# Routing 13 sequences ahead of the attention, and the experts' sums beside its last steps

## The chip, the cores and the metric

The kernel runs on one core of a Trainium2 chip. Measured is the device time of one execution, in microseconds; given is the median over runs. The core's engines are TensorE (PE in the profile; PEld are its weight loads), VectorE (DVE), ScalarE (ACT), GpSimd (POOL) and SyncE (SP). Each works through its own list of instructions in order, and they wait for one another by semaphores. SyncE only issues transfers here; GpSimd and ScalarE can issue some too. All transfers run on the core's 16 DMA engines.

## The reference, cut to what matters

Two layers follow each other on 32 sequences of 256 tokens with 128 features. Layer 0 (a Mamba block and a gated feed-forward) is not touched. Layer 1 adds two results to the stream x, both computed from the same normalised x:

```python
xn = _layernorm(x, axis=-1)
x = x + _L1_attn_ref(xn, ...) + _L1_ffn_ref(xn, wg, we)

def _L1_attn_ref(...):          # 16 heads of 8 features, queries and keys through a latent, rotary half
    ...
    scores = jnp.where(causal[None, None], scores, -jnp.inf)
    att = jax.nn.softmax(scores, axis=-1)
    y = jnp.einsum('bhqk,bhkd->bhqd', att, v)
    return y.transpose(0, 2, 1, 3).reshape(b, t, c) @ Wc

def _L1_ffn_ref(x, wg, we):     # 128 experts, 32 places in each, two experts per token
    xt = x.reshape(-1, d)
    logits = xt @ wg
    gates = jax.nn.softmax(logits, axis=-1)
    ...                         # e1, e2: best and second expert; loc1, loc2: running counts over all tokens
    buf = buf.at[idx1].add(xt * v1[:, None])
    buf = buf.at[idx2].add(xt * v2[:, None])
    yb = jnp.einsum('ecd,edf->ecf', buf.reshape(E, C, d), we).reshape(E * C, d)
    y = (g1 * v1)[:, None] * yb[idx1] + (g2 * v2)[:, None] * yb[idx2]
    return y.reshape(B, S, d)
```

A token's place at its expert depends on the counts of all tokens, so no expert can begin before all 32 sequences are routed. Attention has no such tie between sequences.

## The kernel before

Layer 1 is one block in which each engine runs the same loop over steps (`schedule`), with `now` from -24 to 420. Every operation has a fixed step. The tables `PE_AT`, `ACT_AT`, `DVE_AT`, `POOL_AT` and `SP_AT` give it relative to its sequence's start, and the order of the `for` loops in an engine's `half` gives the order within one step. Nothing is rearranged at run time: an engine that waits holds up all that it has queued.

Attention of sequence n starts at step 12 n (`HS1` = 12), so twelve steps are one sequence. Over some 60 steps a sequence passes these stages. TensorE makes queries, keys, their rotary parts and values (lines 1437, 1442, 1455); VectorE, GpSimd and ScalarE rotate them and split them in bf16 parts (lines 1728, 1732, 1621 to 1627, 1573); SyncE stores the parts and loads them in another order. A first pass in six units (lines 1367, 1374) computes scores into S1, and VectorE takes the negative row maxima (line 1808, one per unit). The maxima are split in three bf16 parts (lines 1716 to 1722), transposed (1425), copied (1552), and go through DRAM into rows of QS (SyncE, lines 1289 and 1294). A second pass in six units (1387, 1394) computes scores less maxima into S2, and ScalarE takes the exponential (1567). TensorE multiplies by the values (1409, 1411); ScalarE copies (1561); TensorE transposes (1511); VectorE divides (1791, 1793); and through lines 1516, 1556 and 1521 comes the product with Wc, which VectorE adds to X (line 1800) at step 12 n + 43. S1 and S2 hold one unit each.

Routing of a sequence runs ahead of its attention. Its steps are counted from `routing(n)`: normalising and transposing (1616, 1618, 1431, 1540), the logits (1450), the two best experts (1737, 1740), one-hot masks and running counts (1746, 1464, 1465, 1548, 1754), and a table of places (1759, 1636, 1471, 1765).

```python
def routing(n):
    return max(HS1 // 2 * n, HS1 * (n - AHEAD))
```

Two sequences are routed in twelve steps until one is AHEAD sequences in front, then one in twelve. The last one is routed at `MAPPED` = HS1 * (NSEQ - 1 - AHEAD). Then totals are taken and places decoded on VectorE, and from `GATHER` = MAPPED + 8 on, one of eight batches of 16 experts starts every 10 steps: GpSimd gathers token rows (1647), TensorE transposes them (1490) and multiplies them with the experts' weights (1497), ScalarE scales by the gate (1588), GpSimd scatters the rows to a DRAM array y (1655). Batch b's scaling is at GATHER + 10 b + 9, its scatter at + 11.

At the steps FINAL[g], SyncE loads the results of 1024 tokens of group g (two loads of 512 KB, first and second expert) into one of two buffers YC; g = 0 first waits for all scatters. Eight steps later VectorE adds both to X (lines 1816 and 1818), after the attention's addition to the same rows. Eleven steps later SyncE stores 512 KB to the output. Before, FINAL runs from 376 to 398; the last attention starts at step 372 and ends at 415.

Of the kernel before, what the change touches and what calls it, by code (L numbers as in the profile page):

```python
# [13 lines left out]
P = 128  # L14
NTOK = 32 * 256
NT = NTOK // P
D = 128
# [998 lines left out]
J1 = L // P  # L1016
NSEQ = NTOK // L
# [8 lines left out]
LEAD = 4  # L1026
UNITS = 6
HS1 = 2 * UNITS
AHEAD = 7
RING = AHEAD + BUF + 1  # L1030
NG, NV, BATCHES = E1 * CAP // P, 2, 8
YBUF, WBUF = 4, 3
# [40 lines left out]
def layer1(nc, ctx, t, dram, scratch, out):  # L1073
# [18 lines left out]
    def sb(name, shape, dt=F32):  # L1092
        return ctx.enter_context(nc.sbuf_tensor(name, shape, dt))
# [7 lines left out]
    X, ident, identb, iota = t["X"], t["ident"], t["identb"], t["iota"]  # L1101
# [23 lines left out]
    dec = sb("dec_1", [P, 3, CAP]); empty = sb("empty_1", [P, CAP]); second = sb("second_1", [P, CAP])  # L1125
    idx = sb("idx_1", [P, 2, NG], U32); sgn = sb("sgn_1", [P, NG]); wsl = sb("wsl", [P, 2, 4])
    XG = sb("XG", [P, 2, 4, D + 1]); XGT = sb("XGT", [P, 4, P]); YB = sb("YB", [P, YBUF, 4, D])
    WE = sb("WE", [P, WBUF, 16, D]); YC = sb("YC", [P, 2, 2, 8, D])
    zeros = sb("zeros", [P, 2 * NTOK * D // (P * NSEQ)])
    S1 = ctx.enter_context(nc.psum_tensor("S1", [P, 2, 512], F32))  # L1130
    S2 = ctx.enter_context(nc.psum_tensor("S2", [P, 2, 512], F32))
# [43 lines left out]
    parts_d, nm_d, xn_d, y_d = scratch["parts"], scratch["nm"], scratch["xn"], scratch["y"]  # L1175
# [7 lines left out]
    MAPPED = HS1 * (NSEQ - 1 - AHEAD)  # L1183
    GATHER = MAPPED + 8
    EVERY = 10
    FINAL = (376, 378, 381, 384, 389, 392, 395, 398)

    def schedule(eng, half):

        for now in range(-24, HS1 * (NSEQ + 3)):
            def due(at):
                if (now - at) % HS1 == 0 and 0 <= (now - at) // HS1 < NSEQ:
                    n = (now - at) // HS1
                    yield n, n % BUF

            def ahead(at):
                for n in range(NSEQ):
                    if routing(n) + at == now:  # L1200
                        yield n, n % BUF

            half(due, ahead, now)

    def routing(n):

# [17 lines left out]
    def batch(at, now):  # L1224

        if (now - GATHER - at) % EVERY == 0 and 0 <= (now - GATHER - at) // EVERY < BATCHES:
            yield (now - GATHER - at) // EVERY
# [5 lines left out]
    def _(sp):  # L1233
# [8 lines left out]
        for s in (parts_out, parts_in, nm_out, nm_in):  # L1242
            sp.sem_inc(s.sem, LEAD * s.per)

        yv, ov = y_d.rearrange("(c i p) d -> p c i d", c=2, p=P), out.rearrange("(i p) d -> p i d", p=P)

        def weights(b):
            if b >= WBUF:
# [17 lines left out]
        def half(due, ahead, now):  # L1266
# [27 lines left out]
                    sp.dma_start(QS[64 * r + KQ + 2:64 * r + KQ + 5, m].rearrange("p i t -> p (i t)"),  # L1294
                                 nm_d[m].rearrange("(x r i) t -> r x (i t)", x=3, r=2)[r]).then_inc(nm_in.sem, 16)

            for g in range(8):
                if now == FINAL[g]:
                    if g == 0:
                        for i in range(YBUF):  # L1300
                            sp.wait_ge(scattered[i], 16 * NG // YBUF)
                    if g >= 2:
                        sp.wait_ge(added, g - 1)
                    for c in range(2):
                        sp.dma_start(YC[:, g % 2, c, :, :], yv[:, c, 8 * g:8 * g + 8, :]).then_inc(y_loaded[g % 2], 16)
                if g < 7 and now == FINAL[g] + 11:
                    sp.wait_ge(added, g + 1)
                    sp.dma_start(ov[:, 8 * g:8 * g + 8, :], X[:, 8 * g:8 * g + 8, :]).then_inc(stored, 16)

        schedule(sp, half)  # L1310
        sp.wait_ge(added, 8)
        sp.wait_ge(x_upd.sem, x_upd.at(NSEQ - 2, 1))
        sp.dma_start(ov[:, 56:62, :], X[:, 56:62, :]).then_inc(stored, 16)
        sp.wait_ge(x_upd.sem, x_upd.at(NSEQ - 1, 1))
        sp.dma_start(ov[:, 62:64, :], X[:, 62:64, :]).then_inc(stored, 16)
        sp.wait_ge(stored, 16 * 9)

    @block.tensor
    def _(pe):
# [207 lines left out]
    def _(act):  # L1527
# [3 lines left out]
        nc.scalar.activation(wsl[:, 0, 0:1], ident[:, 0:1], ACT.Sqrt)  # L1531
        act.wait_ge(stat_step, 7)
        nc.scalar.activation(stats[:, :, 0], q1[:], ACT.Sqrt).then_inc(root_done, 1)

        def half(due, ahead, now):
            for n, m in ahead(ACT_AT["xT"]):
# [31 lines left out]
            for k in range(2):  # L1568
                for n, m in due(ACT_AT["spl"][k]):
# [2 lines left out]
                        act.wait_ge(parts_out.sem, parts_out.at(n - 1, 96))  # L1572
                    nc.scalar.copy(SPL[:, k], (QK if k == 0 else R1)[:]).then_inc(part_done.sem, 1)  # L1573

            for b in batch(6, now):
                act.wait_ge(grouped, b + 1)
                if b:
                    act.wait_ge(applied, b)
                nc.scalar.copy(XGT[:].rearrange("p k q -> p (k q)"), ACC[:]).then_inc(tr_copied, 1)
                act.wait_ge(weighed, 3 * b + 1)  # L1580
                nc.scalar.activation(wsl[:, b % 2], wsl[:, b % 2], ACT.Exp).then_inc(wexp, 1)
# [79 lines left out]
    def _(dve):  # L1661
# [48 lines left out]
        def half(due, ahead, now):  # L1710
# [83 lines left out]
                                            ALU.mult).then_inc(epi.sem, 1)  # L1794
            for n, m in due(DVE_AT["x"]):
                dve.wait_ge(ep_wc.sem, ep_wc.at(n, 1))
                if n == NSEQ - 1:
                    dve.wait_ge(added, 8)
                xs = X[:, n * J1:n * J1 + J1, :]
                nc.vector.tensor_tensor(xs, EP[:, 0:L].rearrange("p (j d) -> p j d", j=J1), xs, ALU.add).then_inc(x_upd.sem, 1)  # L1800
            for u in range(UNITS):
# [7 lines left out]
                                            S1[:].rearrange("p r (j k) -> p r j k", j=wide_), AX.X, ALU.max, negate=True).then_inc(max_done.sem, 1)  # L1809

            for g in range(8):
                if now == FINAL[g] + 8:
                    dve.wait_ge(x_upd.sem, x_upd.at(min(4 * g + 3, NSEQ - 2), 1))
                    dve.wait_ge(y_loaded[g % 2], 32 * (g // 2 + 1))
                    x = X[:, 8 * g:8 * g + 8, :]
                    nc.vector.tensor_tensor(x, YC[:, g % 2, 0], x, ALU.add).then_inc(half_added, 1)
                    dve.wait_ge(half_added, g + 1)
                    nc.vector.tensor_tensor(x, YC[:, g % 2, 1], x, ALU.add).then_inc(added, 1)
# [87 lines left out]
```

## Time and profile before

| what | value |
|---|---|
| median of 3 runs | 2105.19 us (2105.03 to 2108.21) |
| profiled execution, its own time | 2106.87 us |
| its span, first to last instruction | 2105.0 us |
| mean granted TensorE clock | 0.957 |
| layer 1 in the span | about 1436 to 2105 us |
| busy: TensorE, VectorE, ScalarE, GpSimd | 1905.6, 1680.0, 1337.3, 1308.6 us |

All rows are from one profiled execution and count from its span's start. Busy is the time in which an engine worked on instructions; matmuls overlap one another, so that the distance from one group's start to the next is shorter than the length shown. A bracket behind a row is the idle time of that engine just before it, and what ended it. The granted clock is a share of full speed, 2.4 GHz.

### The profile page before, as it was taken

To read this page: it belongs to the slowest core of one execution; us is meant where nothing else is said; L and a number is where in the kernel's file an instruction comes from. 1 tells how busy PE (TensorE), PEld (TensorE's weight loads), DVE (VectorE), ACT (ScalarE), POOL (GpSimd) and SP (SyncE) were. 2 spreads that over 40 slices of the span, in tenths; PEclk is the share of its full clock that TensorE was granted. 3 is DMA by queue.
4 is the path that set the end of the run, shared out by engine and by line. 5 is a ranking of instruction groups with operands and counts; after the bars stand their busy time and mean duration, and the time that the engine had idled before them with its cause. 6 is when DMAs were issued, how large, how long until landed. Compare 5 with 4: busy or idle time off the path is not lost. (4 is left out here: it accounts for less than half of the span.)

```text
span 2105.0 us, 39182 instructions
## 1 busy us (share of the span) xinstructions
PE 1905.6 (91%) x14386; PEld 1117.0 (53%) x14386; DVE 1680.0 (80%) x2731; ACT 1337.3 (64%) x2423; POOL 1308.6 (62%) x1005
## 2 busy tenths in 40 slices
PE   5789999999999999999999999994899999998984
PEld 3445555555555555555555555553455555554542
DVE  5588889898888887988989879884888777776655
ACT  3577776776777767767777677651455555554652
POOL 2577877868778788688787787863433333333660
PEclk7899999999999999999999999995899999998997
DMA  8633615425336154263360632606444444445558
GB/s 201 154 85 72 140 42 122 106 47 145 80 78 141 34 130 101 52 141 78 86 139 24 141 90 57 141 6 169 118 124 112 115 118 118 117 135 144 176 142 243
DMA packets 211994, 234.89 MB, mean 112 GB/s; under 512 B 31590, under 2 KB 150414, under 8 KB 207694
## 3 DMA queue, kind: packets, MB, share of 16 engines
q1 hardware_dynamic: 207116, 227.98, 43.3%
q0 software_dynamic: 2048, 4.18, 0.7%
q8 instruction: 115, 1.88, 0.4%
q14 instruction: 75, 0.61, 0.1%
q10 hardware_dynamic: 2640, 0.24, 0.1%
HBM read 165.51 MB, written 66.85 MB: 110 GB/s over the span
## 5 line engine op out<-in xcount | busy, mean ns | idle before, releaser
L731 POOL TENSOR_TENSOR dBx<-REP,BC 128x1024 f32<-128x1024 f32 x256 | 603.8, 2362 | 251.8 <-DVE dA L904 221.8
L904 DVE TENSOR_TENSOR_SCAN dA<-dA,dBx 128x512 f32<-128x512 f32 x512 | 626.1, 1223 | 154.3 <-POOL dBx L731 105.9
L403 PE MATMUL UP<-xnT,W 128*128 128x512 f32 x1024 | 517.3, 622 | 51.0 <-ACT hT L605 45.4
L412 PEld LDWEIGHTS DN<-W,hT 128*128 128x128 f32 x4096 | 469.5, 192 | 97.7 <-issue 67.8
L412 PE MATMUL DN<-W,hT 128*128 128x128 f32 x4096 | 495.1, 278 | 0.3 <-ACT GD L612 0.3
L596 ACT ACTIVATE dA<-REP,A 128x512 f32<-128x512 f32 x512 | 354.1, 695 | 88.1 <-DVE PR L913 80.5
L605 ACT ACTIVATE hT<-UP,b 128x512 f32<-128x512 f32 x512 | 355.4, 694 | 67.1 <-PE UP L403 61.6
L913 DVE TENSOR_TENSOR PR<-dA,BC 128x512 f32<-128x512 f32 x512 | 353.6, 691 | 16.0
L403 PEld LDWEIGHTS UP<-xnT,W 128*128 128x128 f32 x1024 | 179.1, 194 | 288.7 <-issue 163.6
L1808 DVE TENSOR_REDUCE NM<-S 128x4 f32<-128x1024 f32 (+1 forms) x192 | 234.1, 1219 | 78.1 <-PE S L1353 77.9
L1567 ACT ACTIVATE PT<-S 128x1024 f32<-128x1024 f32 x192 | 197.2, 1027 | 93.7 <-PE S L1353 93.6
L612 ACT ACTIVATE GD<-DN,gate 128x128 f32<-128x128 f32 x512 | 145.2, 366 | 125.0 <-PE DN L412 124.1
L741 POOL TENSOR_TENSOR FF<-FF,GD 128x512 f32<-128x512 f32 x128 | 163.1, 1275 | 6.1 <-ACT GD L612 6.1
L424 PE MATMUL YS<-PR,fold 128*32 128x512 f32 x1024 | 139.3, 617 | 0.5 <-DVE PR L913 0.5
L1621 POOL TENSOR_TENSOR t<-t 128x512 f32<-128x512 f32 x32 | 40.7, 1271 | 136.0 <-DVE t L1732 135.9
L1548 ACT COPY CS<-ACC 128x256 f32<-128x256 f32 x64 | 23.8, 372 | 102.9 <-PE ACC L1465 102.9
L1409 PE MATMUL OT<-PT,V 128*9 128x256 f32 x1024 | 84.2, 390 | 5.3 <-ACT PT L1567 5.2
L1627 POOL TENSOR_TENSOR SPL<-t,SPL 128x512 bf16<-128x512 f32 x32 | 37.1, 1159 | 73.0 <-ACT SPL L1573 73.0
L970 DVE SCALAR_TENSOR_TENSOR xch<-FRO,convw,xch 128x510 f32<-128x510 f32 (+2 forms) x93 | 69.2, 744 | 8.6 <-ACT xch L655 6.4
L1561 ACT COPY OSB<-OT 128x512 f32<-128x512 f32 x64 | 37.5, 586 | 58.2 <-PE OT L1411 56.9
L424 PEld LDWEIGHTS YS<-PR,fold 128*32 128x32 f32 x1024 | 20.4, 109 | 101.8 <-issue 61.7
L797 POOL TENSOR_TENSOR xch<-xch,soft 128x1024 f32<-128x1024 f32 x16 | 37.6, 2352 | 43.0 <-DVE soft L979 43.0
(251 smaller groups left out, 2648.7 us busy)
## 6 DMA issues: line engine op xcount, KB each, us to landing
BC<-s_b SPq DMA_DIRECT2D x128, 256.0 KB, 5.8
REP<-s_dx SPq DMA_DIRECT2D x124, 256.0 KB, 7.4
REP<-s_delta SPq DMA_DIRECT2D x124, 256.0 KB, 8.8
s_parts<-SPL SPq DMA_DIRECT2D x64, 192.0 KB
KS<-s_parts SPq DMA_DIRECT2D x64, 192.0 KB
QS<-s_parts SPq DMA_DIRECT2D x64, 192.0 KB
s_dx<-tz SPq DMA_DIRECT2D x16, 512.0 KB, 3.1
s_y<-zeros SPq DMA_DIRECT2D x32, 256.0 KB, 2.8
```

What stands on the lines that cost most here:

```text
L403: nc.tensor.matmul(UP[k % 2][:], W1[:, e % E0, f * P:(f + 1) * P], xnT[:, q, :], start=True, stop=True).then_inc(upf.sem, 1)
L412: last = nc.tensor.matmul(DN[:, j * P:(j + 1) * P], hT[:, e % 2, f, j * P:(j + 1) * P], W2[:, e, f, :], start=(f == 0), stop=(f == FB - 1))
L424: last = nc.tensor.matmul(YS[CB * j:CB * j + CB, :], fold[:], PR[:, (DB * b + j) % (2 * DB), :], start=(q == 0), stop=(q == NQ - 1), tile_ ...
L596: nc.scalar.activation(dA[:, k % 3, :], DR[:, h, j, :], ACT.Exp, scale=A[:, h, j, q:q + 1]).then_inc(da_ready.sem, 1)
L605: nc.scalar.activation(hT[:, e % 2, f, :], UP[k % 2][:], ACT.Relu, bias=b1[:, e % E0, f:f + 1]).then_inc(relu_done.sem, 1)
L612: last = nc.scalar.activation(GD[:, e % 2, j, :], DN[:, j * P:(j + 1) * P], ACT.Copy, scale=gate[:, par, j, e:e + 1])
L731: nc.gpsimd.tensor_tensor(dBx[:, s % 2], DX[:, h, j:j + 2, :], BC[:, q // 2, q % 2, :].unsqueeze(1).to_broadcast([P, 2, T0]), ALU.mult).th ...
L741: nc.gpsimd.tensor_tensor(FF[:, par], FF[:, par], GD[:, e % 2], ALU.add).then_inc(acc_done.sem, 1)
L904: nc.vector.tensor_tensor_scan(h, h, dBx[:, k // 2 % 2, k % 2, :], 0.0, ALU.mult, ALU.add).then_inc(scan_done.sem, 1)
L913: nc.vector.tensor_tensor(PR[:, k % (2 * DB), :], dA[:, k % 3, :], BC[:, q // 2, 2 + q % 2, :], ALU.mult).then_inc(prod_done.sem, 1)
L1567: nc.scalar.activation(PT[:, u // 3, u % 3, :], S2[:].rearrange("p b w -> p (b w)"), ACT.Exp, scale=SCALE).then_inc(exp_done.sem, 1)
L1808: nc.vector.tensor_reduce(NM[:, 0 if a == 0 else 1, :].rearrange("p (r i) -> p r i", r=2)[:, :, heads], S1[:].rearrange("p r (j k) -> p r ...
```

## The change

Routing keeps 13 sequences ahead in place of 7, so `routing(n)` runs two sequences in twelve steps up to n = 26. The ring of transposed inputs (`RING`, xnT) grows with it. MAPPED, GATHER and the batches move with AHEAD. FINAL is now counted from GATHER: 307, 315, ..., 363. The loads of results, and the stores of the first seven groups, move from SyncE's list to ScalarE's, the last thing in a step but for the batches. YC is no buffer of its own any more; it lies on the experts' weights WE. VectorE's sums keep their 8 steps from FINAL. The additions of line 1800 that come after their group's sum wait for it; a sum that comes before some of its group's attention no longer waits for these. A store waits for the sum and for the attention of its group. The last group is stored by SyncE, sequence by sequence.

```diff
-AHEAD = 7
+AHEAD = 13
...
-    WE = sb("WE", [P, WBUF, 16, D]); YC = sb("YC", [P, 2, 2, 8, D])
+    WE = sb("WE", [P, WBUF, 16, D])
+    YC = WE[:].rearrange("p b e d -> p (b e d)")[:, 0:2 * 2 * 8 * D].rearrange("p (g c i d) -> p g c i d", g=2, c=2, i=8)
...
-    FINAL = (376, 378, 381, 384, 389, 392, 395, 398)
+    FINAL = tuple(GATHER + EVERY * (BATCHES - 1) + 13 + 8 * g for g in range(8))
+    SUMMED = 8
...
+    def updated(n):
+        return HS1 * n + DVE_AT["x"]
+
+    def told_out(g):
+
+        return max(FINAL[g] + SUMMED, updated(4 * g + 3)) + 2
...
-            for g in range(8):
-                if now == FINAL[g]:
-                    if g == 0:
-                        for i in range(YBUF):
-                            sp.wait_ge(scattered[i], 16 * NG // YBUF)
-                    if g >= 2:
-                        sp.wait_ge(added, g - 1)
-                    for c in range(2):
-                        sp.dma_start(YC[:, g % 2, c, :, :], yv[:, c, 8 * g:8 * g + 8, :]).then_inc(y_loaded[g % 2], 16)
-                if g < 7 and now == FINAL[g] + 11:
-                    sp.wait_ge(added, g + 1)
-                    sp.dma_start(ov[:, 8 * g:8 * g + 8, :], X[:, 8 * g:8 * g + 8, :]).then_inc(stored, 16)
-
         schedule(sp, half)
         sp.wait_ge(added, 8)
-        sp.wait_ge(x_upd.sem, x_upd.at(NSEQ - 2, 1))
-        sp.dma_start(ov[:, 56:62, :], X[:, 56:62, :]).then_inc(stored, 16)
-        sp.wait_ge(x_upd.sem, x_upd.at(NSEQ - 1, 1))
-        sp.dma_start(ov[:, 62:64, :], X[:, 62:64, :]).then_inc(stored, 16)
-        sp.wait_ge(stored, 16 * 9)
+        for n in range(NSEQ - 4, NSEQ):
+            sp.wait_ge(x_upd.sem, x_upd.at(n, 1))
+            sp.dma_start(ov[:, n * J1:n * J1 + J1, :], X[:, n * J1:n * J1 + J1, :]).then_inc(stored, 16)
+        sp.wait_ge(stored, 16 * 11)
...
+            for g in range(8):
+                if now == FINAL[g]:
+                    if g == 0:
+                        for i in range(YBUF):
+                            act.wait_ge(scattered[i], 16 * NG // YBUF)
+                    if g >= 2:
+                        act.wait_ge(added, g - 1)
+                    for c in range(2):
+                        act.dma_start(YC[:, g % 2, c, :, :], yv[:, c, 8 * g:8 * g + 8, :]).then_inc(y_loaded[g % 2], 16)
+                if g < 7 and now == told_out(g):
+                    act.wait_ge(added, g + 1)
+                    act.wait_ge(x_upd.sem, x_upd.at(4 * g + 3, 1))
+                    act.dma_start(ov[:, 8 * g:8 * g + 8, :], X[:, 8 * g:8 * g + 8, :]).then_inc(stored, 16)
...
-                if n == NSEQ - 1:
-                    dve.wait_ge(added, 8)
+                if FINAL[n // 4] + SUMMED < now:
+                    dve.wait_ge(added, n // 4 + 1)
...
-                if now == FINAL[g] + 8:
-                    dve.wait_ge(x_upd.sem, x_upd.at(min(4 * g + 3, NSEQ - 2), 1))
+                if now == FINAL[g] + SUMMED:
+                    for n in range(4 * g + 3, 4 * g - 1, -1):
+                        if updated(n) <= now:
+                            dve.wait_ge(x_upd.sem, x_upd.at(n, 1))
+                            break
```

## Rows read from the trace of the kernel before

**Rows 1.** Busy time by stage: stretch, its length, PE, PEld, DVE, ACT, POOL, PEclk, DMA, GB/s

```profile
1560.90:1581.80 20.90, 19.31 (x237) 11.62 (x236) 18.19 (x54) 10.93 (x20) 6.79 (x9) 1.00 0.39 111
...
1617.10:1879.90 262.80, 253.94 (x3306) 150.71 (x3300) 209.97 (x526) 149.21 (x240) 90.95 (x105) 1.00 0.43 117
...
1941.98:2011.96 69.98, 65.29 (x974) 39.37 (x976) 44.76 (x85) 43.13 (x78) 50.45 (x49) 1.00 0.64 187
...
2050.56:2105.03 54.47, 27.08 (x320) 14.13 (x316) 28.46 (x40) 16.39 (x21) 2.71 (x3) 0.73 0.80 237
...
2071.10:2089.00 17.90, 13.38 (x150) 6.42 (x150) 8.65 (x13) 8.17 (x10) 0.00 (x0) 0.68 1.01 297
```

**Rows 2.** Timeline of VectorE, line 1800: sequences 1, 2, 20, 26, 27 and 28

```profile
1560.88 0.42 DVE L1800 TENSOR_TENSOR X<-EP,X 128x256 f32<-128x256 f32 x1
1581.84 0.42 DVE L1800 TENSOR_TENSOR X<-EP,X 128x256 f32<-128x256 f32 x1
...
1896.89 0.41 DVE L1800 TENSOR_TENSOR X<-EP,X 128x256 f32<-128x256 f32 x1
...
2011.96 0.39 DVE L1800 TENSOR_TENSOR X<-EP,X 128x256 f32<-128x256 f32 x1
2036.05 0.41 DVE L1800 TENSOR_TENSOR X<-EP,X 128x256 f32<-128x256 f32 x1
2050.56 0.41 DVE L1800 TENSOR_TENSOR X<-EP,X 128x256 f32<-128x256 f32 x1
```

**Rows 3.** Timeline of TensorE at the end: start, length, what, idle time before

```profile
2073.07 0.61 PE L1387 MATMUL S<-QS,KS 53*128 53x128 bf16 x8 [10.03 <-DMA QS<-s_nm]
...
2089.56 0.63 PE L1511 MATMUL EP<-ident,OSB 128*128 128x128 f32 x4 [1.34 <-DVE X L1800]
...
2098.17 1.11 PE L1511 MATMUL EP<-ident,OSB 128*128 128x128 f32 x4 [7.98 <-DVE YN L1793]
```

**Rows 4.** Timeline of TensorE, one period beside the expert batches

```profile
1976.01 0.40 PE L1367 MATMUL S<-KS,QS 50*128 50x128 bf16 x8
...
1976.58 0.70 PE L1442 MATMUL FR<-xnT,wqr 128*128 128x256 f32 x2
...
1977.64 0.64 PE L1409 MATMUL OT<-PT,V 128*9 128x256 f32 x8
...
1978.93 0.66 PE L1490 MATMUL ACC<-ident,XG 128*128 128x128 f32 x4
1979.52 0.39 PE L1374 MATMUL S<-KS,QS 50*128 50x256 bf16 x4
...
1981.75 1.08 PE L1497 MATMUL ACC<-WE,XGT 128*32 128x128 f32 x32
1982.65 0.63 PE L1409 MATMUL OT<-PT,V 128*9 128x256 f32 x8
...
1985.43 0.40 PE L1367 MATMUL S<-KS,QS 50*128 50x128 bf16 x8 [0.27 <-DVE NM L1808]
...
1986.31 0.28 PE L1425 MATMUL FR<-identb,NMS 128*128 128x128 bf16 x2 [0.25 <-DVE NMS L1722]
...
1993.94 0.40 PE L1367 MATMUL S<-KS,QS 50*128 50x128 bf16 x8
```

**Rows 5.** VectorE: the first sum, and a maximum in the batches (timeline)

```profile
1991.40 1.23 DVE L1808 TENSOR_REDUCE NM<-S 128x4 f32<-128x1024 f32 x1 [1.29 <-PE S L1353]
...
2060.69 1.22 DVE L1816 TENSOR_TENSOR X<-YC,X 128x1024 f32<-128x1024 f32 x1 [2.39 <-DMA YC<-s_y]
2061.95 1.22 DVE L1818 TENSOR_TENSOR X<-YC,X 128x1024 f32<-128x1024 f32 x1
```

**Rows 6.** Line 1305 on SyncE: issue in ns min/median/max, first and last start; landing

```profile
L1305 SPq DMA_DIRECT2D YC<-s_y x16: 359/584/2404, 2055.2 to 2089.5; - x16
...
DMA to landing us min/median/max: 3.8/5.3/8.0
```

**Rows 7.** Timeline of ScalarE, the scaling of the last expert batch

```profile
2047.16 1.16 ACT L1588 ACTIVATE YB<-ACC,wsl 128x128 f32<-128x128 f32 x4
```

More of the change, by code:

```diff
@@ L1243, in _ @@
             sp.sem_inc(s.sem, LEAD * s.per)
-        yv, ov = y_d.rearrange("(c i p) d -> p c i d", c=2, p=P), out.rearrange("(i p) d -> p i d", p=P)
+        ov = out.rearrange("(i p) d -> p i d", p=P)
         def weights(b):
@@ L1533, in _ @@
         nc.scalar.activation(stats[:, :, 0], q1[:], ACT.Sqrt).then_inc(root_done, 1)
+        yv, ov = y_d.rearrange("(c i p) d -> p c i d", c=2, p=P), out.rearrange("(i p) d -> p i d", p=P)
         def half(due, ahead, now):
```

## The prediction

> **What bounds the kernel now.** I went first to the table of stages, then to the times at which each sequence of layer 1 finishes, then into single steps. I write x(n) for the addition that finishes sequence n (line 1800); it stands at step 12n+43 of the written-out order, so two neighbouring x are 12 steps apart, and their distance is the pace.
>
> TensorE sets the pace of layer 1. In the stretch of fifteen sequences that each carry one routing it is busy 253.94 of 262.8 us, 97%, at granted clock 1.00, the 2.4 GHz level; VectorE has 80%, ScalarE 57% [rows 1]. A sequence there takes 262.8/15 = 17.52 us; with two routings beside it 20.96, TensorE busy 19.31 of 20.90 [rows 1, 2]. So most work that moves keeps its price, and what can be won or lost is TensorE's idle time. That lies at the end: after x(28) TensorE works 27.08 of 54.47 us at a mean clock of 0.73 [rows 1]. Three of its waits there are long. Sequence 31's second pass waits 10.03 us for its maxima, which SyncE stored and loaded behind its own loads of the experts' results. Then 1.34 and 7.98 us go on the last transposes, because VectorE stands in the eight sums, which wait for those loads [rows 3]. The reader should see that all of that is the price of doing the sums last.
>
> **The change, step by step.** AHEAD 7 to 13 makes routing run at double pace for 72 steps more. MAPPED goes from step 288 to 216, and the expert batches, GATHER + 10b, from 296 to 224. 72 is six times 12, so every batch instruction meets the same phase of the attention as before, six sequences earlier. FINAL was 376 to 398 and becomes 307, 315, ..., 363; each sum comes 8 steps later, the last at 371, before x(28) at 379.
>
> I build the new time on the old x. Up to x(2), 1581.84, nothing differs [rows 2].
>
> - Double pace: x(3) to x(8) at 20.96 each: 1581.84 + 125.8 = 1707.6.
> - Single pace: before, x(2) to x(20) is 315.05 us; twelve of these eighteen go, at 17.52: 104.8 stay, x(14) at 1812.4. The two together cost TensorE little idle time: six sequences of 1.6 us more, twelve of 0.6 less.
> - Totals, decoding, batches: old x(20) to x(26), 115.07 us, is repeated: x(20) at 1927.5.
> - Old x(26) to x(28) took 24.09 and 14.51 [rows 2]. These had no q, k and rotary products of a following sequence; now they do. The rotary pair takes 1.06 us from its start to that of the next product (1976.58 to 1977.64) [rows 4], the q and k pair of the same shape as much: 2.1 in each. So 26.2 + 16.6: x(22) at 1970.3. The last two batches share GpSimd's queue with the rotary additions of two more sequences (line 1621); the batches before them did that too, at the same phases, so their pace holds the price. Here all batches are done.
> - Attention alone, x(22) to x(27). The trace has no such stretch. One period in the batches, from one first pass of the second half-group to the next, is 1993.94 - 1976.01 = 17.93 us; in it lie two transposes of expert rows (0.59 to the next start) and one expert product (0.90). Without them 15.85 [rows 4]. Four sequences with their batches take 69.98 us; a batch comes every 10 steps, so 4.8 batches of 1.5 us lie in these 48 steps: (69.98 - 7.2)/4 = 15.7. TensorE's busy time alone gives (65.29 - 7.2)/4 = 14.5 [rows 1]. I take 15.7, because waits for VectorE's maxima (0.27, 0.25 us) are in the period and don't go away when there is less to do between [rows 4]. Five: 78.5, x(27) at 2048.8. Bounds 14.5 and 15.9.
> - x(28): old 14.51 less one batch's 1.5 gives 13.0; I take 13.2. 2062.0.
> - The end: old 54.47 less the three waits: 35.1 [rows 1, 3]. It can be shorter by some 2 us if the clock stays at 2.4 GHz, or longer if TensorE falls to 1.2 GHz as it did after the 10 us wait. Without anything for the sums: 2097.1.
>
> So moving the work gains 8 us, and the sums, loads and stores beside steps 307 to 371 have to be paid from it.
>
> *Sums on VectorE.* Two additions of 1.22 us for each of eight groups [rows 5]: 2.45 us in one piece ahead of everything that VectorE has queued. Counted in steps of 12, they stand at 3, 11, 7, 3, 11, 7, 3, 11. At 11 the next thing in the queue is the split of the maxima (line 1716), and TensorE's transpose of it already waits for it now, 0.25 us in [rows 4]. Three groups therefore cost their full 2.45: 7.4 us. At 3 and 7 VectorE next waits for a first pass; it idled 1.29 us at step 3 [rows 5], so the next maximum is some 1.2 us late and TensorE feels part of it. Between nothing and 1.2 I take 0.5, five times: 2.5.
>
> *Loads and stores on ScalarE's queue.* An issue took 0.359 us at least and 0.584 in the middle [rows 6], a pair about 1.0, a store the same again by half. That would be 12 us of ScalarE, but ScalarE idles 43% [rows 1], some 7.5 us in each sequence, in gaps of 1.2 us and more between six exponentials. The issues stand at odd steps, exponentials at even ones: nearly all hidden; 1 us taken, and 12 if no gap fits. The first load also waits for the last scatter. Before, the first issue came at 2055.2, 6.9 us after the last expert scaling on ScalarE ended (2047.16 + 1.16) [rows 6, 7]. ScalarE now comes to the wait four steps after that scaling, having spent some 4 us; it stands still 3 us with the exponentials queued behind, and TensorE loses about 2. Bounds 0 and 6.9.
>
> *SyncE* loses the loads and seven stores; its maxima exchange no longer stands behind them. The alias of YC on WE waits for nothing new, since the scatters come after the last expert product. The final stores are four of 128 KB, only the last one after the end of x(31), as now.
>
> The DMA engines reached a share of 1.01 at 297 GB/s from 2071 to 2089 [rows 1]. New traffic: 12 MB of loads and stores in 64 steps of about 86 us, 140 GB/s, beside 117 GB/s of a sequence with its routing [rows 1], which are fewer without: under 257 GB/s, below that full rate. Loads landed after 3.8 to 8.0 us [rows 6], eight steps are 10.5. I charge nothing more. The Trainium skill, DMA: Bandwidth & Descriptors, section "Issuing engines are not separate DMA queues", says that transfers issued from ScalarE or SyncE run on the same 16 DMA engines and interleave, so that a second issuing engine saves only the issue time. In layer 1 this trace has loads on SyncE's queue alone, so no row here shows it; by that rule the loads still compete with the attention's own transfers, which is the third rival below.
>
> Sum: 2097.1 + 7.4 + 2.5 + 1 + 2 = 2110.0, against the profiled span of 2105.0: 5.0 us more, which on the median of 2105.19 is **2110.2 us**. (The profiled execution itself took 2106.87, 1.9 us more than its span and 1.7 above the median.) A measurement tells 0.2%, 4.2 us, from no change, so this stands only just outside.
>
> **Rivals.** Each in the median's terms.
>
> 1. *The sums are hidden* (faster). Place: VectorE's queue at steps 307 to 371. TensorE waits in an attention-only sequence anyway, 15.7 against 14.5 us busy; if the delay of a sum falls on those waits, it costs nothing. 2110.2 - 9.9 - 2 (the scatter wait hidden in the same way) = 2098.3. It decides from 0.6 us per group down: eight of them and the 3 us of ScalarE are then less than the 8 won. Against it: the split of the maxima has no slack.
> 2. *Attention alone runs at TensorE's busy time*, 14.5 in place of 15.7: 2110.2 - 6.0 = 2104.2, no change. For it: VectorE and ScalarE lose the routing's work as well. Against: the single period, which has the waits in it [rows 4].
> 3. *The transfers collide.* The exchange of the maxima is a store and a load in a row; one that stood behind loads cost 10.03 us [rows 3]. On another queue I put it at a tenth, eight times: 2118.
> 4. *ScalarE's queue becomes the bound.* The longest issue took 2.404 us [rows 6]. If every second issue on ScalarE takes that long and the others 0.4, a group's three take 4.2 us in two gaps of 1.25; 1.7 stay over, eight times: 2124. Against it: that issue followed others on its own queue; ScalarE's has three in eight steps.
>
> **From these to the numbers.** The forecast has 0.52, its own range 2104 to 2116 (step price 15.5 to 15.9: 2 us; end 33 to 37; sums 4 us); of this 0.33 lies beyond 2109.4, 0.18 within 0.2%, 0.01 below. Rival 1 has 0.20 (0.15 faster, 0.05 same), rival 2 0.10 (0.03, 0.07), rival 3 0.10 and rival 4 0.08, both slower. Faster 0.19, same 0.30, slower 0.51. From 2097 to 2120 all but some 0.15 lies inside: rival 4 and the ends of 1 and 3 are left out.
>
> **What the changed profile would show.** Right, if x(8) comes near 1708, x(14) near 1812, x(22) near 1970, and x(28) at 2070 to 2076 with 33 to 37 us after it; TensorE's transposes at line 1425 wait near 2.4 us behind the sums of groups 1, 4 and 7; no long wait for the maxima's load or for line 1793 remains at the end. Five sequences at 14.5 us speak for rival 2, at 15.7 with no wait of line 1425 for rival 1. Waits of TensorE for QS from nm or parts between 1970 and 2060 speak for rival 3, waits of line 1387 and 1394 for line 1567 just behind ScalarE's issues for rival 4. I am wrong at the root if x(22) is off by more than 5 us: then double pace, or the batches six sequences earlier, don't cost what they did.

## The result, and the profile after

The change makes the kernel slower: a median of 2138.76 us (2127.42 to 2142.96, four executions) against 2106.70 in the same comparison, a ratio of 1.0140, 95% interval 1.0121 to 1.0160. Forecast were 2110.2 us, at most 2120. The direction was right, the size was not. The profiled execution of after is the fastest of the four: 2127.42 us, span 2125.6, granted clock 0.953. The other three had clocks of 0.941 to 0.950 and spans up to 2141.2. So the rows of after show the loss at its smallest, some 11 us below the median.

First the forecast's milestones, the timeline of VectorE in after, sequences 8, 14, 22, 27 and 28; the line of [rows 2] is now 1809:

```profile
1705.00 0.42 DVE L1809 TENSOR_TENSOR X<-EP,X 128x256 f32<-128x256 f32 x1
...
1809.72 0.41 DVE L1809 TENSOR_TENSOR X<-EP,X 128x256 f32<-128x256 f32 x1
...
1965.94 0.42 DVE L1809 TENSOR_TENSOR X<-EP,X 128x256 f32<-128x256 f32 x1
...
2065.99 0.41 DVE L1809 TENSOR_TENSOR X<-EP,X 128x256 f32<-128x256 f32 x1
...
2089.69 0.42 DVE L1809 TENSOR_TENSOR X<-EP,X 128x256 f32<-128x256 f32 x1
```

Up to x(0) the two kernels do the same work, and this execution was 2.6 us ahead there (x(0) at 1537.29 against 1539.91). With these 2.6 us added back, x(8) is at 1707.6 (forecast 1707.6), x(14) at 1812.3 (1812.4), x(22) at 1968.5 (1970.3). Double pace, single pace and the batches cost what the rows of before said. From x(28) to the end it is 35.9 (35.1). All that went wrong lies between x(22) and x(28): 123.75 us, where 104.6 were forecast (91.7 without the sums, and 12.9 for sums, loads and stores).

The windows of after show this stretch by sequence; columns as in [rows 1]:

```profile
1965.94:1989.46 23.52, 18.04 (x222) 10.10 (x220) 12.81 (x21) 9.85 (x14) 5.76 (x6) 0.85 0.59 158
...
2009.01:2026.58 17.57, 15.44 (x222) 8.88 (x220) 15.15 (x22) 9.39 (x14) 3.58 (x3) 1.00 0.87 229
...
2065.99:2089.69 23.70, 20.11 (x200) 9.42 (x202) 11.52 (x19) 8.32 (x11) 0.00 (x0) 0.57 0.29 71
2089.69:2125.60 35.91, 24.82 (x328) 13.24 (x326) 9.23 (x24) 16.38 (x21) 0.00 (x0) 0.88 0.06 17
...
1965.94:2089.69 123.75, 101.30 (x1210) 53.90 (x1210) 81.13 (x117) 53.88 (x76) 20.18 (x18) 0.82 0.65 173
```

The eighth column is the one to read. The stretch ran at a mean granted clock of 0.82, and the sequence before x(28) at 0.57, near the 1.2 GHz level. TensorE is *busy* for 20.11 us there with 200 products; in e1 below, the same stretch of the schedule fills 12.84 us at clock 1.00. Why the clock fell is seen in the timeline of TensorE, its longest waits in this stretch (the bracket is the idle time before the row):

```profile
1974.20 1.12 PE L1506 MATMUL EP<-ident,OSB 128*128 128x128 f32 x4 [4.56 <-ACT OSB L1557]
...
2001.00 0.29 PE L1420 MATMUL FR<-identb,NMS 128*128 128x128 bf16 x2 [3.06 <-DVE NMS L1731]
...
2035.82 0.61 PE L1362 MATMUL S<-KS,QS 50*128 50x128 bf16 x8 [1.86 <-DMA QS<-s_parts]
...
2038.13 0.39 PE L1420 MATMUL FR<-identb,NMS 128*128 128x128 bf16 x2 [1.34 <-DVE NMS L1731]
2038.45 1.06 PE L1404 MATMUL OT<-PT,V 128*9 128x256 f32 x8
...
2066.45 0.61 PE L1382 MATMUL S<-QS,KS 53*128 53x128 bf16 x8 [1.95 <-DMA QS<-s_nm]
...
2080.97 0.40 PE L1420 MATMUL FR<-identb,NMS 128*128 128x128 bf16 x2 [2.43 <-DVE NMS L1731]
2081.30 1.06 PE L1404 MATMUL OT<-PT,V 128*9 128x256 f32 x8
```

Three kinds of stop: one for ScalarE, which stood at the first load until the last scatter had landed; three for the split of the maxima, which stands behind a sum on VectorE; two for score operands that came late through DRAM. And the products behind the stops are long: the one with the values took 1.06 us, where it takes 0.64 at the high level [rows 4].

### The profile page after: what moved, and what is told of

Read it like the earlier page. It is cut to its first block and busy times, and to the rows that moved or that the text cites. A ratio compares the mean times of both kernels' runs of the same rounds, so it can differ in the third digit from the quotient of the medians.

```text
span 2125.6 us, 39188 instructions
## 1 busy us (share of the span) xinstructions
PE 1921.6 (90%) x14386; PEld 1120.3 (53%) x14386; DVE 1686.5 (79%) x2731; ACT 1340.5 (63%) x2423; POOL 1305.7 (61%) x1005
## 5 line engine op out<-in xcount | busy, mean ns | idle before, releaser
L1817 DVE TENSOR_REDUCE NM<-S 128x4 f32<-128x1024 f32 (+1 forms) x192 | 234.0, 1219 | 91.9 <-PE S L1348 91.7
```

Of the source, the lines that this page charges most:

```text
L1817: nc.vector.tensor_reduce(NM[:, 0 if a == 0 else 1, :].rearrange("p (r i) -> p r i", r=2)[:, :, heads], S1[:].rearrange("p r (j k) -> p r ...
```

## The experiments

Ratios are to the kernel before, measured beside each run on the same chip, with their 95% intervals. After itself, to compare with, is 1.0140 (1.0121 to 1.0160). Each run has one traced execution, and that can lie some us off the run's median.

**e1: without loads and sums.** What does the move cost before the sums have a price?

```diff
-                if now == FINAL[g]:
...
-                        act.dma_start(YC[:, g % 2, c, :, :], yv[:, c, 8 * g:8 * g + 8, :]).then_inc(y_loaded[g % 2], 16)
...
-                    nc.vector.tensor_tensor(x, YC[:, g % 2, 0], x, ALU.add).then_inc(half_added, 1)
...
+                    nc.vector.tensor_copy(cnt[:], bit[:, 0:1]).then_inc(added, 1)
```

> Leaves out the loads of the experts' results and both additions to X (one tiny copy stands for each sum); the stores stay. My sum without anything for the sums was 2097.1 us of span, and the changed kernel's own profile agrees with it up to x(22). Theory (the moved routing gains what was forecast; the loss comes from the loads, the sums and the waits for them): span 2094 to 2100, about 2096 to 2102 us. Rival (attention without routing beside it is itself slower than the 15.7 us per sequence taken): 2110 us or more, with x(22) to x(27) above 16.5 us each.

Measured: 2101.13 us, 0.9973 (0.9963 to 0.9983). The windows of e1, the stretch from x(22) to x(28) in one row, and its last sequence:

```profile
1971.58:2065.36 93.78, 85.60 (x1218) 48.82 (x1216) 61.30 (x108) 53.69 (x76) 20.09 (x18) 1.00 0.53 138
2050.50:2065.36 14.86, 12.84 (x200) 7.05 (x196) 9.36 (x17) 8.11 (x11) 0.00 (x0) 1.00 0.36 97
```

The moved work is worth what was forecast, less 2 us: attention alone takes (2050.50 - 1971.58)/5 = 15.8 us a sequence at clock 1.00. The first row is also the measure for after's. From 93.78 to 123.75 are 30.0 us: TensorE is idle 22.45 in place of 8.18 us, 14.3 more, and busy 101.30 in place of 85.60 us, 15.7 more, with as many products (1210 against 1218 in the records). So the stops themselves cost about what I charged (12.9). The other half is the same products at a lower clock: e1's row stands at 1.00, after's at 0.82.

**e4: dummy products in the stops.** This tests the clock directly: 70 extra bf16 products into a spare bank while TensorE waits.

```diff
+        def warm(k):
+            for i in range(k):
+                nc.tensor.matmul(ACC[:, 0:2 * P], identb[:], maskq[:].rearrange("p a b -> p (a b)"), start=True, stop=True)
...
+            if now == FINAL[0]:
+                pe.wait_ge(yb_done, BATCHES)
...
+                if now - 1 in [f + SUMMED for f in FINAL]:
+                    warm(14)
                 pe.wait_ge(nm_step.sem, nm_step.at(n, 4))
...
+                        if now == FINAL[0] + 1:
+                            warm(28)
                         pe.wait_ge(ot_copied.sem, ot_copied.at(n, 2))
```

> As the changed kernel, but TensorE gets work to do where it stood still: 28 matmuls of 256 columns into a bank that is free by then, ahead of the transposes that waited for ScalarE at the first load, and 14 ahead of each of the three transposes that waited for the split of the maxima behind a sum. The waits stay, only the engine is busy in them. Theory (the second half of the loss is the clock that falls to 1.2 GHz after such stops): granted clock near 1.00 from x(22) to x(28) where it was 0.57 to 0.85 in three of six sequences, and 8 to 15 us less, 2123 to 2131 us. Rival (the clock falls for the low share of work in this stage altogether, or costs little): clock as before and the same time or 1 to 2 us more.

Measured: 2122.86 us, 1.0088 (1.0071 to 1.0105). With more work that is 16 us less by the medians, 11 us by the ratios (0.52%). The windows of e4, x(22) to x(28):

```profile
1969.63:2084.56 114.93, 98.04 (x1288) 56.31 (x1286) 80.90 (x117) 53.77 (x76) 20.17 (x18) 0.96 0.68 186
```

The clock went from 0.82 to 0.96. The waits for ScalarE and for the split of the maxima are still there; TensorE only works in part of them. Of its 98.04 busy us the 70 dummies are 8.3, so the kernel's own products took 89.7 us, where after has 101.30 and e1 85.60: 11.6 of the 15.7 us came back. The dummies and the idle time together are 2.7 us more than after's idle time, and the stretch is 8.8 us shorter in these two executions, 114.93 in place of 123.75. That the low clock costs time of its own, beside the stops, is shown; that it is half of the whole loss rests on the rows of after and e1, since e4 gives back 11 to 16 us of 35.

**e5 and e6: loads without sums, sums without loads.** In e5 the same small copy as in e1 stands for a sum; in e6 the loads are left out and the sums read what lies in the buffer. e5, then e6:

```diff
                     dve.wait_ge(y_loaded[g % 2], 32 * (g // 2 + 1))
-                    nc.vector.tensor_tensor(x, YC[:, g % 2, 0], x, ALU.add).then_inc(half_added, 1)
...
+                    nc.vector.tensor_copy(cnt[:], bit[:, 0:1]).then_inc(added, 1)
```

```diff
-                        act.dma_start(YC[:, g % 2, c, :, :], yv[:, c, 8 * g:8 * g + 8, :]).then_inc(y_loaded[g % 2], 16)
...
-                    dve.wait_ge(y_loaded[g % 2], 32 * (g // 2 + 1))
+                    dve.wait_ge(applied, BATCHES)
```

> Leaves out both additions of the experts' results to X (one tiny copy, behind the wait for the load, stands for each); loads, stores and their waits stay on ScalarE's queue. Without loads and sums the kernel took 2101 us, with both 2139. Theory (the stop at the first load, 4.6 us, and collisions of transfers, some 4 us, with a clock stretch behind them; the sums carry the rest): 2108 to 2118 us. Rival (loads and stores on that queue are the main loss, the sums only fall into time that is lost anyway): 2125 us or more.

> Leaves out the loads: the additions run at their steps on what lies in the buffer, without waiting for a load or a scatter; stores stay. Theory: three stops of 2.4 us at line 1725's product, some 2 us at the other five sums, and stretches at 1.2 GHz behind them: 2112 to 2122 us. Rival (a sum alone fits into VectorE's idle time and stops TensorE only together with late transfers): 2106 us or less.

Measured: e5 2122.68 us, 1.0089 (1.0060 to 1.0117); e6 2124.14 us, 1.0087 (1.0072 to 1.0103). Over e1 that is 1.16% and 1.14%, 24 us each; both together, in after, cost 1.67%, 35 us. Each alone already brings some two thirds of the loss, more than expected of either. The timelines of TensorE say why, first e5's longest waits, then e6's:

```profile
1978.99 0.66 PE L1506 MATMUL EP<-ident,OSB 128*128 128x128 f32 x4 [3.73 <-ACT OSB L1557]
...
2020.78 0.61 PE L1362 MATMUL S<-KS,QS 50*128 50x128 bf16 x8 [2.89 <-DMA QS<-s_parts]
...
2072.84 0.61 PE L1362 MATMUL S<-KS,QS 50*128 50x128 bf16 x8 [2.81 <-DMA QS<-s_parts]
```

```profile
1996.60 0.28 PE L1420 MATMUL FR<-identb,NMS 128*128 128x128 bf16 x2 [3.26 <-DVE NMS L1723]
...
2033.68 0.28 PE L1420 MATMUL FR<-identb,NMS 128*128 128x128 bf16 x2 [3.26 <-DVE NMS L1723]
...
2074.13 0.29 PE L1420 MATMUL FR<-identb,NMS 128*128 128x128 bf16 x2 [2.43 <-DVE NMS L1723]
```

Without sums the operands QS are up to 2.9 us late: the loads of results delay the attention's own loads. Without loads the split of the maxima is up to 3.3 us late behind a sum. The two losses don't add up (48 against 35), so in after they must partly cover each other; which wait hides which is not shown.

**e2, e3, e7: one step moved.** Three small edits, one each: the sums two steps later, behind the split of the maxima where they stood ahead of it; the first load five steps later; the stores of seven groups issued by SyncE after the last exchange of maxima.

```diff
-    SUMMED = 8
+    SUMMED = 10
```

```diff
-    FINAL = tuple(GATHER + EVERY * (BATCHES - 1) + 13 + 8 * g for g in range(8))
+    FINAL = tuple(GATHER + EVERY * (BATCHES - 1) + 13 + 8 * g + (5 if g == 0 else 0) for g in range(8))
```

```diff
-                if g < 7 and now == told_out(g):
...
+            if now == HS1 * (NSEQ - 1) + SP_AT["nm_in"] + 1:
+                for g in range(7):
...
+                    sp.dma_start(ov[:, 8 * g:8 * g + 8, :], X[:, 8 * g:8 * g + 8, :]).then_inc(stored, 16)
```

> The sums stand 10 steps after their load in place of 8: at phases 5, 1 and 9 of twelve, none just ahead of the split of the maxima. Theory (three sums ahead of line 1725 stop TensorE for 6.8 us in all, and the stretches at 1.2 GHz behind these stops cost about as much again): 10 to 16 us less than the changed kernel, 2120 to 2129 us. Rival (these waits are a symptom, the time goes with the first load's wait and the transfers): less than 5 us gained, 2133 us or more.

> The first load of results stands 5 steps later (312 in place of 307), its sum at 320, all else as it was: ScalarE should no longer stand still for the last scatter. Theory (that stop cost TensorE 4.6 us and a stretch of 6.9 us at 1.2 GHz behind it): 6 to 9 us less, 2129 to 2133 us. Rival (a stop of ScalarE is made up for later): no change, 2136 to 2141 us.

> The seven stores of 512 KB leave ScalarE's queue and steps 317 to 369; SyncE issues them after the last exchange of maxima, where the DMA engines are at a share of 0.06. Loads and sums as in the changed kernel. Theory (a third of the added traffic goes, and with it the late parts and maxima, 1.9 us each time with a clock stretch behind): 4 to 10 us less than the changed kernel, 2128 to 2135 us. Rival (the late parts come from the loads alone or cost nothing): no change, 2136 us or more.

Measured: e2 2130.63 us, 1.0119 (1.0103 to 1.0136); e3 2130.04 us, 1.0108 (1.0091 to 1.0125); e7 2131.78 us, 1.0122 (1.0107 to 1.0138). The medians are 7 to 9 us below after's, but the intervals overlap after's 1.0121 to 1.0160, and in the one profiled execution of each, x(22) to x(28) still takes 121.3, 123.1 and 127.2 us. So each helps a little at most, and none is told apart from after for certain. The traced executions of e3 and e7 are their slowest (2134.25 and 2136.51 us). The medians of e3 and e7 lie where their theories had them; e2 was to gain 10 us or more and did not. In e2 the waits for NMS are gone, as expected, but waits of 1.3 us for YN and of 1.2 to 1.4 us for QS are there in their place, and the first load still stops TensorE for 4.2 us. In e3 the stop at the first load is gone: x(22) to x(23) takes 15.90 us at clock 1.00, where after has 23.52. But x(23) to x(24) takes 24.27 us at 0.76 in place of after's 19.55. In these executions, taking one of several stops away gave back little.

**e8 and e9: the sums on GpSimd.** Both other costs taken away together: the sums go to GpSimd (2.35 us for an addition, in three buffers, group 7 first), the stores to SyncE at the end, and the first load comes 6 steps later. In e8 loads stand where buffers come free; in e9 mostly one step into a sequence, away from the loads of KS and QS.

```diff
+    ORDER = (7, 0, 1, 2, 3, 4, 5, 6)
+    LOAD = (313, 319, 325, 343, 355, 361, 371, 375)     # e9: (313, 325, 337, 349, 361, 369, 371, 375)
+    SUM = (327, 339, 351, 363, 367, 371, 378, 382)      # e9: (327, 339, 351, 363, 367, 375, 379, 383)
...
+                    nc.gpsimd.tensor_tensor(x, YC[:, s % 3, 0], x, ALU.add).then_inc(half_added, 1)
+                    pool.wait_ge(half_added, s + 1)
+                    nc.gpsimd.tensor_tensor(x, YC[:, s % 3, 1], x, ALU.add).then_inc(added, 1)
```

> GpSimd does the sums in place of VectorE, three at its idle steps 327, 339, 351, the others from 363 on, when it has nothing else to do (3.6 of 17 us busy per sequence now); three buffers of results in place of two, the first load 6 steps later, stores as in the late-stores kernel. Theory (the loss is VectorE's queue, ScalarE's stop and the collisions, with the clock behind each): all of it goes, 2101 to 2106 us, equal to the kernel before or up to 0.2% faster. Rival (any work beside attention alone costs, since two engines' access or the transfers slow it): 2112 us or more.

> As the run with GpSimd's sums (2109.5 us, 1.002 of before), but the loads of the results are issued one step into a sequence each (steps 313, 325, 337, 349, 361, 369, 371, 375 in place of 313, 319, 325, 343, 355, 361, 371, 375), away from the loads of the score operands (QS, KS). Theory (what is left of the loss there is the collision of the two kinds of load, and the stretch at 1.2 GHz behind each wait for QS): the waits for QS of 1.62 and 2.51 us go to under 0.5, the sequences from x(22) to x(27) take about 16 us each as in the run without sums, and the time is 2099 to 2105 us, 0.997 to 0.9995 of before. Rival (GpSimd's sums hold up its part of the routing and the exchange, whatever the loads do): waits of 1 to 3 us stay, on other tiles than QS, and the time stays at 2107 to 2112 us.

Measured: e8 2109.52 us, 1.0021 (1.0006 to 1.0036); e9 2108.82 us, 1.0005 (0.9993 to 1.0016). Nearly all of the loss is gone, but the 6 us that e1 has over before are not there. The windows of e8 around one load of results show one more cause, and behind them stands TensorE's wait in its timeline. This execution is the slowest of e8's eleven (2119.70 us):

```profile
1990.00:1997.00 7.00, 5.31 (x76) 3.13 (x74) 4.11 (x10) 4.57 (x7) 3.14 (x3) 0.95 1.05 278
1997.00:2007.00 10.00, 9.58 (x81) 4.41 (x78) 3.67 (x3) 3.26 (x5) 4.84 (x3) 0.50 0.54 159
```

```profile
1996.59 0.61 PE L1364 MATMUL S<-KS,QS 50*128 50x128 bf16 x8 [1.62 <-DMA QS<-s_parts]
```

The DMA engines are at their full share (1.05 at 278 GB/s) while a load of results and the loads of KS and QS are on their way; TensorE waits 1.62 us for QS at 1996.59, and the next 10 us run at clock 0.50, 1.2 GHz. In e9 x(22) to x(27) takes 79.75 us, within 1 us of e1, and clock 1.00 holds; e8's execution took 91.04. So the traces bear the collision out for that stretch, though the medians of e8 and e9 are 0.7 us apart and their intervals overlap. The expected 2099 to 2105 us was missed: two loads still stood beside the last operands, QS came 2.72 us late there, and at the same time the issue of these loads held ScalarE for 4.45 us.

**e10 and e11: the last loads, and the last sums.** e10 issues the last three loads behind the last operands; e11 also holds GpSimd's last three sums until VectorE has split the last maxima.

```diff
-    LOAD = (313, 325, 337, 349, 361, 369, 371, 375)
-    SUM = (327, 339, 351, 363, 367, 375, 379, 383)
+    LOAD = (313, 325, 337, 349, 361, 374, 377, 381)
+    SUM = (327, 339, 351, 363, 367, 378, 382, 386)
...
+                    if s >= 5:                                   # e11 only
+                        pool.wait_ge(nm_step.sem, nm_step.at(NSEQ - 1, 4))
```

> As the run before, but the last three loads of results are issued at steps 374, 377 and 381 in place of 369, 371 and 375, so that they go out when the score operands of the last sequence have landed, and their sums on GpSimd at 378, 382 and 386. In the run before, the stretch from x(22) to x(27) was already that of the run without sums (79.8 us), and 5.9 of its 6.6 us over that run lay behind x(27), where the loads of 369 and 371 stood beside those of KS and QS (wait of 2.72 us for QS). Theory (collision, nothing else): the wait for QS before the last sequence falls from 2.72 to about 1.2 us (that of the run without sums), x(27) to the end takes 51 to 53 us in place of 56.6, and the time is 0.997 to 0.999 of before (2100 to 2105 us). Rival (the sums at the end cost as such): x(27) to the end stays at 56 us or more, 1.000 of before or above.

> As the run before, but GpSimd's last three sums also wait for the last sequence's split of the maxima on VectorE. In the run before, the waits for QS went to 0.43 us and x(28) - x(27) to 14.9 us, as the collision theory has it, but a new wait of 6.65 us for NMS came in the last sequence: three of VectorE's four small operations of the split (0.18 to 0.19 us each otherwise) took 1.66, 2.20 and 2.27 us while GpSimd's sums ran back to back from 2068.8 to 2083 us. Theory (the two engines take turns on operations whose operands all lie in SBUF, so that a small operation of VectorE waits for the end of a GpSimd one): the four operations take 0.2 us each again, the wait for NMS falls to about 1.1 us, x(29) - x(28) from 21.5 to about 14 us, and the time falls by 6 to 8 us, to 0.9975 to 0.9995 of before (2101 to 2105 us). Rival (the split is late for another reason, the loads of the results for one): the operations stay long or the wait stays over 4 us, and the time stays at 1.001 or above.

Measured: e10 2111.00 us, 1.0019 (1.0009 to 1.0029); e11 2105.05 us, 0.9993 (0.9983 to 1.0003). In e10 the wait for QS fell to 0.43 us and x(27) to x(28) to 14.94 us, as e1 has it, and a wait of 6.65 us for the split of the maxima came in its place. The expected 2100 to 2105 us was missed, and the rival's sign came: 57.3 us from x(27) to the end. The timelines of TensorE, VectorE and GpSimd in e10:

```profile
2080.71 0.39 PE L1422 MATMUL FR<-identb,NMS 128*128 128x128 bf16 x2 [6.65 <-DVE NMS L1739]
```

```profile
2072.97 1.23 DVE L1825 TENSOR_REDUCE NM<-S 128x4 f32<-128x1024 f32 x1 [0.69 <-PE S L1350]
2074.23 1.66 DVE L1733 CAST NMS<-NM 128x32 bf16<-128x32 f32 x1
2075.92 0.19 DVE L1735 TENSOR_TENSOR NR<-NM,NMS 128x32 f32<-128x32 f32 x1
2076.15 2.20 DVE L1737 CAST NMS<-NR 128x32 bf16<-128x32 f32 x1
2078.39 2.27 DVE L1739 TENSOR_TENSOR NMS<-NR,NMS 128x32 bf16<-128x32 f32 x1
```

```profile
2073.50 2.35 POOL L1671 TENSOR_TENSOR X<-WE,X 128x1024 f32<-128x1024 f32 x1
2075.93 2.38 POOL L1673 TENSOR_TENSOR X<-WE,X 128x1024 f32<-128x1024 f32 x1
2078.27 2.33 POOL L1671 TENSOR_TENSOR X<-WE,X 128x1024 f32<-128x1024 f32 x1
```

The small operations take 0.18 to 0.19 us elsewhere; here three of them end within 0.1 us of the end of a GpSimd sum (2075.85, 2078.31, 2080.60), and the one that started in the gap between two sums took its 0.19. The maximum ahead of them, which reads S from PSUM, kept its 1.23 us. The timelines of VectorE and TensorE in e11:

```profile
2073.34 0.18 DVE L1735 CAST NMS<-NM 128x32 bf16<-128x32 f32 x1
2073.55 0.19 DVE L1737 TENSOR_TENSOR NR<-NM,NMS 128x32 f32<-128x32 f32 x1
2073.78 0.18 DVE L1739 CAST NMS<-NR 128x32 bf16<-128x32 f32 x1
2073.99 0.19 DVE L1741 TENSOR_TENSOR NMS<-NR,NMS 128x32 bf16<-128x32 f32 x1
```

```profile
2074.24 0.28 PE L1422 MATMUL FR<-identb,NMS 128*128 128x128 bf16 x2 [1.07 <-DVE NMS L1741]
```

The four operations are back at 0.2 us each, the wait for NMS is 1.07 us, and x(28) to x(29) takes 13.2 us in place of 21.5. The time fell by 6 us, as expected if the two engines take turns. e11 is not told apart from before; no version here is clearly faster than before but e1, which lacks the sums.

## Why the prediction was right and wrong

**The base was right.** Double pace, single pace, the batches, the 35 us at the end and the 15.7 us of attention alone came out within 2 us each. One part of this is luck. The 24.09 us of old x(26) to x(27) are not all work: the timeline of TensorE in before has a stop of 5.12 us in them, and the window of 2023.6 to 2031.6 us stands at clock 0.57.

```profile
2024.65 0.61 PE L1387 MATMUL S<-QS,KS 53*128 53x128 bf16 x8 [5.12 <-ACT PT L1567]
```

After has the same stop six sequences earlier (5.05 us, at 1937.15, and 0.57 from 1936.1 to 1944.1 us), so the old time, clock and all, still came near: 24.59 us, where 26.2 were forecast. e1 puts the gain without sums at 5.7 us (forecast: 8). Rival 2 is refuted by e1's 15.8 us.

**The stops were sized about right, in sum.** Three sums at step 11: 7.4 us charged; after's waits for the split are 3.06, 1.34 and 2.43, 6.8. The wait at the first load: 2 charged, 4.56 measured; ScalarE stood idle 6.27 us, near the upper bound. The transfers: nothing charged, 1.86 and 1.95 measured. Together TensorE's idle time grew by 14.3 us over e1, where 12.9 were charged. That the sum fits is luck in part: two terms were too small, and the other five sums and the issues, charged 3.5 us, add next to nothing on top.

**The step that failed is the price of a stop.** I charged each stop its own length, in the sums' term and in the scatter's. In this stretch of after TensorE runs at 1.2 GHz behind its stops of 1.9 to 4.6 us, and products then take up to 1.06 us in place of 0.64: 15.7 us on top, half of the stretch's 30.0. The rows of before had it: clock 1.00 in the full stages and 0.73 at the end, behind waits of up to 10.03 us [rows 1, 3], and the stop of 5.12 us above. I allowed for the clock in the last term alone (some 2 us shorter, or longer), where TensorE was idle anyway, and not where I was adding idle time. By experiment, loads alone, charged 3 us, cost 24 (e5), and sums alone, charged 9.9, cost 24 (e6); e4 got 11 to 16 us back with 70 products that compute nothing. The spread of after's own executions goes with the clock too: spans of 2125.6 to 2141.2 us at 0.953 to 0.941. Only the fastest has a trace, so its cause is not shown.

**Rival 3 was half right.** The transfers do collide, but it was not the exchange of maxima alone, and not by a tenth of 10 us: QS was up to 2.9 us late in e5, the part that comes from s_parts. My argument against it was a mean, 257 GB/s against 297. Within one window of e8 the engines stood at 1.05 and 278 GB/s, and the operands loaded in it were late. This is what the Trainium skill, DMA: Bandwidth & Descriptors, section "Issuing engines are not separate DMA queues", says of transfers issued from two engines, and the traces agree: in e5 the loads of results go out on ScalarE's queue, there are no sums, and the QS that SyncE loads comes up to 2.89 us late, where e1 has 1.19 at most. How much of e5's 24 us is this, and how much the stop of 3.73 us at the first load, is not told apart. That layer 1 of before has loads on SyncE's queue alone was a misreading: GpSimd issues the gathers of XG there.

**Rivals 1 and 4 are refuted.** The sums are not hidden: e6 is 24 us above e1. ScalarE's queue is not the bound in after: but for the first load, no issue there made ScalarE wait, for a reason that I had not seen, below. In e8, e9 and e11 single issues did.

What stays open: how the 15.7 us of clock are shared among single stops. e2 and e3 each took one kind away and moved the time by no more than the measurement tells, so the parts don't add. And equal stops don't cost the same. e6 has two of 3.26 us; the windows behind them:

```profile
1997.00:2000.10 3.10, 3.10 (x30) 1.12 (x22) 1.16 (x2) 1.23 (x3) 0.00 (x0) 0.50 0.62 177
2034.00:2044.50 10.50, 10.08 (x90) 5.18 (x89) 4.81 (x6) 3.33 (x6) 0.00 (x0) 0.52 0.61 158
```

About 3 us at the low level follow the first, about 10 the second, and their sequences take 19.52 and 21.38 us, where e1's take 15.9. Why is not shown.

## What to carry to other kernels

Price a stop of TensorE in a full stretch at about twice its length until a row shows that the clock holds: here 30.0 us were lost for 14.3 us of added idle time, single stops costing less or more. Expect little from taking away one of several stops. A time that is read off as elapsed may already hold a stop with its clock. Compare transfers not by their mean rate over a stage but by what is in flight while a load with a deadline is: from e8 to e9 five loads of results moved by a few steps, and the waits for QS of 1.62 and 2.51 us went. Before moving elementwise work to another engine, look which small operations on the path run beside it.

## What the runs showed of the hardware

*ScalarE issues a transfer while it computes.* The timeline of ScalarE in after, the first load, and an exponential with a later pair of loads:

```profile
1972.44 1.02 ACTq L1579 DMA_DIRECT2D WE<-s_y  x2
1973.56 0.59 ACT L1557 COPY OSB<-OT 128x512 f32<-128x512 f32 x1 [6.27 <-issue]
...
1983.69 1.02 ACT L1563 ACTIVATE PT<-S 128x1024 f32<-128x1024 f32 x1 [0.24 <-PE S L1348]
1983.77 1.08 ACTq L1579 DMA_DIRECT2D WE<-s_y  x2
```

The later pair's 1.08 us run beside the activation's 1.02, but for 0.14 at the end. So here issuing beside a long activation cost next to nothing. A wait ahead of an issue does cost, as the 6.27 us at the first load show, which stood there for the last scatter. So does an issue that outlasts what runs beside it. In e11 one pair stood beside a copy of 0.37 us and took 2.24 us, where the same pair in e10 took 1.00. The timelines of ScalarE and of TensorE in e11:

```profile
2040.15 2.24 ACTq L1581 DMA_DIRECT2D WE<-s_y  x2
2042.78 0.59 ACT L1559 COPY OSB<-OT 128x512 f32<-128x512 f32 x1 [2.27 <-issue]
```

```profile
2044.43 0.64 PE L1406 MATMUL OT<-PT,V 128*9 128x256 f32 x8 [2.16 <-ACT PT L1565]
```

ScalarE stood for 2.27 us, TensorE then for 2.16, the clock fell, and x(27) to x(28) took 18.44 us in place of e10's 14.94. In e8 one pair of 2.08 us held ScalarE for 1.81 us, and TensorE waited 1.70. What makes an issue long is not shown.

*VectorE and GpSimd take turns.* Shown in e10 and e11: an operation of 0.19 us took up to 2.27 us while a GpSimd sum ran. The same is seen twice in after, where two of the sixteen additions took 2.06 us in place of 1.23 (at 1998.13 and 2035.26, over GpSimd operations that ended at 1999.10 and 2036.24). The Trainium skill, SBUF — State Buffer, section "Who interferes with whom", calls the shared port pair of the two engines an exclusive lock; these rows agree. Operations that read from PSUM were not held up: the maximum kept its 1.23 us, the division that follows its 0.29 (at 2080.86 in e10, beside a sum).
